# A two-layer adapter and feed-forward kernel: the second gate/up tile as seven block products instead of full ones

## The chip, the cores and the metric

The kernel runs on one core of one Trainium2 chip. The metric is the device time of one execution in microseconds (us), lower is better; a run's figure is the median of several executions. TensorE multiplies matrices into PSUM (eight banks of 128 x 512 float32), VectorE and ScalarE work elementwise on SBUF and PSUM, GpSimd works elementwise on SBUF and issues the gathers, and SyncE issues most of the other DMAs. Each engine takes its own list of instructions strictly in order and waits on semaphores for the others.

## What is computed

Two layers act on x, 8 x 128 tokens of width 512, in float32:

```python
def reference(x, itok_B_0_7, itok_B_3_7, ...):
    x = x + _L0_ffn_ref(_L0_cond_ref(x, itok_B_0_7, ...), ...)   # part touched here: _L0_ffn_ref
    x = x + _L1_ffn_ref(_L1_cond_ref(x, L1_cond_weight, itok_B_3_7), ...)
    return x
...
def _L0_ffn_ref(x, qweight_gu, qzeros_gu, scales_gu, g_idx_gu, ...):
    w_gu = _dequant(qweight_gu, qzeros_gu, scales_gu, g_idx_gu)   # sc[g] * (wq - (zq[g] + 1)), 4 bits
    inter = jnp.einsum('bsh,hf->bsf', x, w_gu)
    gate, up = (inter[..., :INTER], inter[..., INTER:])           # INTER = 1376
    h = jax.nn.silu(gate) * up
    w_d = _dequant(qweight_down, qzeros_down, scales_down, g_idx_down)
    return jnp.einsum('bsf,fh->bsh', h, w_d)
```

`_L0_cond_ref` is a linear layer with two gated low-rank experts for each token; its result is called y below. Layer 1 has the same shape with unquantized weights.

## The kernel before

**Three matmuls for one.** Every float32 operand is kept as a rounded high part (suffix `_hi`, made by a ScalarE copy) and the rest (`_lo`, made by a VectorE subtraction from it). A product of a 128 x 128 weight tile with 512 tokens is three matmuls of 512 columns: hi x hi, hi x lo, lo x hi.

**Gate/up of layer 0.** The 1376 hidden features make 11 tiles of 128 (`FT0 = 11`), numbered 0 to 10. A tile's weights are 128 gate and 128 up columns against 512 inputs. Tiles in `PLAIN` (0 and 1) are full products: `gate(i)` and `up(i)`, 4 input blocks x 2 token halves x 3 matmuls = 24 each. Tiles in `BLOCK_TILES` (2 to 10) treat weights and y as 2 x 2 blocks and take seven block products (a Winograd scheme) where eight are needed: `y_p_1` to `y_p_7`, each 2 x 3 = 6 matmuls, 42 a tile. Their right operands are blocks of y or of four sums of y's blocks (`yt_hi`, `yt_lo`, numbered 1 to 4), their left ones blocks of the weights or of four sums, which GpSimd makes for each tile (`sums_gu(i)`, four additions of 128 x 256).

**What a block tile costs the other engines.** VectorE dequantizes the raw weights (`dequant_gu(i)`, line 1252), GpSimd makes the sums, ScalarE rounds them (`w_hi(i)`, two copies, 768 and 1024 columns), VectorE makes the low part (`w_lo(i)`, lines 1241 and 1121). While TensorE runs the products, ScalarE takes three snapshots of banks (`y_snap_1`, `_5`, `_2`), VectorE adds other banks to them (`y_c_11`, `y_c_12`, `y_c_22`, lines 1291, 1296, 1301), ScalarE applies silu, and VectorE multiplies the two token halves (`y_mul_1` line 1311, `y_mul_0` line 1306). `h_split(i)` makes the high (ScalarE) and low (VectorE) part of the hidden tile. A plain tile needs one silu and one `gate_times_up` (line 1281) for these. Banks alternate between 0 to 3 and 4 to 7. TensorE's order in a tile i is p1(i), p4(i-1), p5, p2, p6, p3, p7; p4(i-1) waits for `y_c_22(i-1)`, which stands behind p7(i-1), and p1(i) for `w_lo(i)`.

**Order by hand.** Each engine's list is written out in its own function: nothing reorders it. The four differences of y (lines 1342 to 1348) are made on VectorE from `y_raw`, ScalarE's copies of the banks in which y's four quarters were summed (`y_copy`), and split by `y_sum_hi` and `y_sum_lo`. Zero points arrive by gather (`zg`) and are added to the 4-bit values for groups of tiles (`add_zeros`, line 1225; `ZERO_PARTS`). Scales arrive by four gathers for each pair of tiles (`scales_gu(j)` for tiles 2j and 2j+1). GpSimd's list is gathers and additions in one order; a gather for a reused buffer waits for the dequantization that read it.

## Time and profile before

| | |
|---|---|
| median of 3 runs | 441.03 us (440.88 to 444.47) |
| the profiled execution's own time | 440.44 us |
| its span, first to last instruction | 438.6 us |
| busy: TensorE matmul / VectorE / ScalarE / GpSimd | 99% / 76% / 51% / 48% of the span |
| granted TensorE clock, mean | 1.000 |
| instructions | 5493, of them 1938 matmuls |

The profile is one execution. A row of its timeline gives an instruction's start and duration and, in brackets, how long its engine had sat idle and what ended that. Matmuls are pipelined: the ends are modelled (390 ns for one of 512 columns), and the distance from start to start is what one costs. On VectorE and ScalarE too the next instruction starts some 0.08 us before the end of the one ahead. GpSimd's spans are rough.

### The profile page before, as it was taken

The numbers are of one execution on the slowest core, as the hardware profiler recorded it, in microseconds if no ns is written. First come the engines' busy times: TensorE is split into PE (matmuls) and PEld (weight loads), VectorE is DVE, ScalarE is ACT, GpSimd is POOL, SyncE is SP. The second block draws the span as 40 slices with busy tenths as digits, with TensorE's granted clock in tenths as the row PEclk, the third lists the DMA queues.
The fourth block names the chain that finished last, engine by engine and source line by source line (L and its number), as shares of the span: only waits on it lengthen the run. The fifth ranks groups of instructions, "written<-read, shape, count | busy, mean of one in ns | idle before, by whom it ended". The sixth has DMA issues, their size and how long they took to land.

```text
span 438.6 us, 5493 instructions
## 1 busy us (share of the span) xinstructions
PE 434.4 (99%) x1938; PEld 354.9 (81%) x1938; DVE 334.1 (76%) x413; ACT 223.8 (51%) x301; POOL 209.8 (48%) x182
## 2 busy tenths in 40 slices
PE   8999999999999999999999999999999999999997
PEld 4788888887888888888888888888888888888886
DVE  4869998999888854646778568778687678999922
ACT  5407646655555443255667756466465654473200
POOL 0477978868888304300024787986987300000000
PEclk9999999999999999999999999999999999999999
DMA  8974044101226475675289427838469136986623
GB/s 287 242 240 132 1 131 150 50 1 19 25 24 156 108 250 230 251 277 191 97 284 374 158 95 231 295 134 277 166 220 306 54 114 263 369 278 189 224 94 143
DMA packets 29401, 78.20 MB, mean 178 GB/s; under 512 B 2432, under 2 KB 15888, under 8 KB 27712
## 3 DMA queue, kind: packets, MB, share of 16 engines
q1 hardware_dynamic: 25312, 66.07, 43.3%
q0 software_dynamic: 3488, 11.10, 9.4%
q10 hardware_dynamic: 576, 0.72, 0.5%
q8 instruction: 13, 0.21, 0.2%
q14 instruction: 12, 0.10, 0.1%
HBM read 57.15 MB, written 20.73 MB: 178 GB/s over the span
## 4 chain that ended last, share of the span: by engine, by line
PE 96%; DVE 2%; DMA 1%; issue 0%; ACT 0%; ACTq 0%; DVEq 0%
PE ps L1937 10%; PE ps L1939 10%; PE ps L1938 10%; PE ps L1682 8%; PE ps L1686 8%; PE ps L1683 8%; PE ps L1805 6%; PE ps L1807 6%; PE ps L1806 6%; PE ps L2052 5%; PE ps L2050 5%; PE ps L2051 5%; PE ps L1920 2%; PE ps L1918 2%; PE ps L1919 2%; DMA res<-in_xT 1%
## 5 line engine op out<-in xcount | busy, mean ns | idle before, releaser
L1937 PE MATMUL ps<-zt_hi,ring_hi 128*128 128x512 f32 x140 | 54.6, 390 | 0.0
L1939 PE MATMUL ps<-zt_hi,ring_lo 128*128 128x512 f32 x140 | 54.5, 389 | 0.0
L1938 PE MATMUL ps<-zt_lo,ring_hi 128*128 128x512 f32 x140 | 54.5, 389 | 0.0
L760 ACT ACTIVATE ring_hi<-raw 128x1792 fp32r<-128x1792 f32 (+2 forms) x32 | 38.7, 1237 | 19.4 <-PE ps L1939 10.2
L1121 DVE TENSOR_TENSOR ring_lo<-raw,ring_hi 128x1024 fp32r<-128x1024 f32 (+3 forms) x24 | 42.4, 1771 | 6.9 <-ACT ring_hi L760 6.9
L1682 PE MATMUL ps<-h_hi,d_hi 128*128 128x512 f32 x88 | 34.2, 389 | 0.0
L1683 PE MATMUL ps<-h_lo,d_hi 128*128 128x512 f32 x88 | 34.2, 389 | 0.0
L670 POOL TENSOR_TENSOR raw<-raw 128x256 f32<-128x256 f32 x21 | 23.9, 1139 | 17.8 <-DMA raw<-in_gu 10.6
L1937 PEld LDWEIGHTS ps<-zt_hi,ring_hi 128*128 128x128 f32 x140 | 26.3, 188 | 6.0 <-issue 0.4
L1939 PEld LDWEIGHTS ps<-zt_hi,ring_lo 128*128 128x128 f32 x140 | 26.3, 188 | 5.5
L1938 PEld LDWEIGHTS ps<-zt_lo,ring_hi 128*128 128x128 f32 x140 | 26.3, 188 | 5.4
L673 POOL TENSOR_TENSOR raw<-raw 128x256 f32<-128x256 f32 x21 | 30.3, 1442 | 0.0
L633 POOL DMA_INDIRECT scale<-in_sc_gu,idx_gu x20 | 26.4, 1322 | 7.2 <-issue 5.3
L1805 PE MATMUL ps<-yt_hi,ring_hi 128*128 128x512 f32 x72 | 28.1, 390 | 0.2 <-DVE snap L1301 0.2
L1686 PE MATMUL ps<-h_hi,w_dn_lo 128*128 128x512 f32 x88 | 28.1, 389 | 0.0
L1807 PE MATMUL ps<-yt_hi,ring_lo 128*128 128x512 f32 x72 | 28.0, 389 | 0.0
L1806 PE MATMUL ps<-yt_lo,ring_hi 128*128 128x512 f32 x72 | 28.0, 389 | 0.0
L2052 PE MATMUL ps<-slot,wd 128*128 128x512 f32 (+1 forms) x73 | 27.8, 380 | 0.0
L2050 PE MATMUL ps<-slot,wd 128*128 128x512 f32 (+1 forms) x73 | 27.8, 380 | 0.0
L676 POOL TENSOR_TENSOR raw<-raw 128x256 f32<-128x256 f32 x21 | 26.1, 1245 | 3.0
L727 POOL TENSOR_TENSOR ad_lo<-ad_raw,ad_hi 128x1024 fp32r<-128x1024 f32 x1 | 2.4, 2405 | 48.6 <-ACT ad_hi L760 48.6
L1530 DVE TENSOR_TENSOR res<-ps,res 128x512 f32<-128x512 f32 (+1 forms) x18 | 10.8, 641 | 15.4 <-PE ps L2052 15.4
(254 smaller groups left out, 1199.8 us busy)
## 6 DMA issues: line engine op xcount, KB each, us to landing
ad_raw<-in_w1T SPq DMA_DIRECT2D x8, 1024.0 KB, 4.7
wd<-down_weights SPq DMA_DIRECT2D x7, 1024.0 KB, 5.5
down_weights<-dhi SPq DMA_DIRECT2D x7, 896.0 KB, 4.6
down_weights<-dlo SPq DMA_DIRECT2D x7, 896.0 KB, 4.1
raw<-in_gu SPq DMA_DIRECT2D x12, 512.0 KB, 3.6
wd<-down_weights SPq DMA_DIRECT2D x7, 768.0 KB, 5.5
draw<-in_d SPq DMA_DIRECT2D x7, 512.0 KB, 4.5
res<-in_xT SPq DMA_DIRECT2D x1, 2048.0 KB, 7.7
```

What stands on the lines that cost most here:

```text
L1121: dve.tensor_tensor(dst, src, hi_part.bitcast(F32), ALU.subtract).then_inc(done_sem, 1)
L1682: pe.matmul(ps[:, bank + hf, :], w_hi, v_hi[:, t], start=first, stop=False)
L1683: pe.matmul(ps[:, bank + hf, :], w_hi, v_lo[:, t], start=False, stop=False)
L1686: ins = pe.matmul(ps[:, bank + hf, :], w_lo, v_hi[:, t], start=False, stop=last)
L1805: pe.matmul(ps[:, bank, :], w_hi, v_hi, start=first_in_bank and k == 0, stop=False, skip_group_check=True)
L1806: pe.matmul(ps[:, bank, :], w_hi, v_lo, start=False, stop=False, skip_group_check=True)
L1807: ins = pe.matmul(ps[:, bank, :], w_lo, v_hi, start=False, stop=k == 1, skip_group_check=True)
L1937: pe.matmul(ps[:, bank, :], ring1_hi[s][:, w], z_hi[:, t], start=first and k == 0, stop=False, skip_group_check=True)
L1938: pe.matmul(ps[:, bank, :], ring1_hi[s][:, w], z_lo[:, t], start=False, stop=False, skip_group_check=True)
L1939: ins = pe.matmul(ps[:, bank, :], ring1_lo[s][:, w], z_hi[:, t], start=False, stop=k == 1, skip_group_check=True)
L2050: pe.matmul(ps[:, bank, c], w_hi, v_hi[:, c], start=k == LAST_K if bank != own else k == 0 and i in (1, 2, 3, 5), stop=False, skip_group_c ...
L2052: return pe.matmul(ps[:, bank, c], w_lo, v_hi[:, c], start=False, stop=k == DH - 1 or (n == 6 and m == 1 and k == LAST_K - 1), skip_group_ ...
```

## The change

Tile 1 moves from `PLAIN` to `BLOCK_TILES`. TensorE runs p1, p2, p5, p6, p3, p7 of tile 1 where `gate(1)` and `up(1)` stood, and its p4 behind p1(2). The weights of tile 1 need sums, so GpSimd gets `sums_gu(1)`; the differences of y, their parts, the combination of tile 1's banks and its multiplications are put in front of tile 2. Around that:

- `add_zeros` for tiles 5 to 10 was one instruction ahead of y's differences; it is now two (tiles 5, 6 and tiles 7 to 10), in the loop of tiles 2 and 3.
- The low part of hidden tile 0 moves into tile 2's loop on VectorE.
- The first adapter low part (`hg_lo`) is made ahead of the first `add_zeros`, and the last two gathers of `scale0` are issued behind the four of `zg`.
- ScalarE splits tile 1's weights behind the last split of y instead of behind the first; VectorE's `w_lo(1)`, `dequant_gu(3)` and the parts of y's sums are in another order. The two added waits on `s_yt` guard a snapshot buffer that shares memory with `y_raw`.
- On GpSimd `scales_gu(4)` waits for four zero parts and stands behind `sums_gu(5)`.

```diff
-BLOCK_TILES = tuple(range(2, FT0))
+BLOCK_TILES = tuple(range(1, FT0))
 NS = len(BLOCK_TILES)
...
 S_COL = {B_S1: 8 * P, B_S2: 10 * P, B_S3: 12 * P}
-PLAIN = (0, 1)
+PLAIN = (0,)
 NPAIRS = FT0 // 2
...
         nib = region(116, "nib", [P, FT0 * 2 * P], F32)
-        sil = {i: region(kb, f"sil{i}", [P, T], F32) for i, kb in zip(PLAIN, (100, 104))}
+        sil = {i: region(kb, f"sil{i}", [P, T], F32) for i, kb in zip(PLAIN, (100,))}
         y_raw = region(184, "y_raw", [P, KD, T], F32)
...
-        ZERO_PARTS = ((0, 2), (2, 5), (5, FT0))
+        ZERO_PARTS = ((0, 2), (2, 5), (5, 7), (7, FT0))
         m16 = nib.bitcast(U16).rearrange("p (i g w) -> p i g w", i=FT0, g=2 * KD)
...
             sp.wait_ge(s_zk, 32)
-            sp.wait_ge(s_ring, len(PLAIN))
+            sp.wait_ge(s_ring, 2)
             sp.dma_start(nib_dn[:, :], a["qw_dn"]).then_inc(s_qd, 16)
...
             pool.wait_ge(s_idx, 2)
-            scale_part(0, 0)
-            for k in range(1, KD):
+            for k in range(2):
                 scale_part(0, k)
...
                 gather(zg[:, 4 * ZW * k:4 * ZW * (k + 1)], kept_z, idx_gu[:, 0, k:k + 1], s_zg)
+            for k in range(2, KD):
+                scale_part(0, k)
...
             scales_gu(1)
+            sums_gu(1)
             scales_gu(2)
...
             sums_gu(4)
+            sums_gu(5)
             pool.wait_ge(s_n, len(ZERO_PARTS))
             scales_gu(4)
-            sums_gu(5)
+            sums_gu(6)
             scales_gu(5)
-            sums_gu(6)
             sums_gu(7)
...
                 act.wait_ge(s_p[1], frame(i) + 1)
+                if i == BLOCK_TILES[0]:
+                    act.wait_ge(s_yt, 3)
                 need(act, s_hm0, frame(i) - 1)
...
                 act.wait_ge(s_p[5], frame(i) + 1)
+                if i == BLOCK_TILES[0]:
+                    act.wait_ge(s_yt, 4)
                 need(act, s_hm1, frame(i) - 1)
...
             y_split(0, 0)
-            w_hi(1)
             y_split(1, 4)
...
             y_split(3, 2)
+            w_hi(1)
             y_copy(3, 2, KD)
...
             y_sum_hi(2)
+            y_sum_hi(3)
             w_hi(2)
-            y_sum_hi(3)
-            y_sum_hi(4)
-            h_split(0)
-            silu(1)
             for i in BLOCK_TILES:
                 y_snap_1(i)
-                if i + 1 < FT0:
+                if i == BLOCK_TILES[0]:
+                    y_sum_hi(4)
+                elif i + 1 < FT0:
                     w_hi(i + 1)
...
                 y_snap_5(i)
-                h_split(i - 1)
+                if i > BLOCK_TILES[0]:
+                    h_split(i - 1)
                 y_snap_2(i)
+                if i == BLOCK_TILES[0]:
+                    h_split(0)
                 y_silu_0(i)
...
                 i0, i1 = ZERO_PARTS[part]
-                dve.wait_ge(s_nib, 2 if i1 == FT0 else 1)
+                dve.wait_ge(s_nib, 2 if i1 > 5 else 1)
                 dve.tensor_tensor(m16[:, i0:i1], m16[:, i0:i1], zg16[:, i0:i1], ALU.add).then_inc(s_n, 1)
...
+            dve.wait_ge(s_hghi, 1)
+            lo(hg_lo, hg_full, hg_hi, s_hglo)
             dve.wait_ge(s_zg, 16 * KD)
             add_zeros(0)
-            dve.wait_ge(s_hghi, 1)
-            lo(hg_lo, hg_full, hg_hi, s_hglo)
             dequant_gu(0)
...
             y_split(0, 0)
-            w_lo(1)
             y_split(1, 4)
...
             dequant_gu(2)
-            y_split(2, 6)
-            y_split(3, 2)
-            dequant_gu(3)
-            add_zeros(2)
             b11, b12 = y_raw[:, 0:2, first], y_raw[:, 0:2, second]
...
             dve.tensor_tensor(y_low(yt_raw, 1), b12, b11, ALU.subtract).then_inc(s_yt, 1)
+            y_split(2, 6)
+            y_split(3, 2)
+            w_lo(1)
             dve.wait_ge(s_yr, KD)
...
             dve.tensor_tensor(y_low(yt_raw, 3), b22, b12, ALU.subtract).then_inc(s_yt, 1)
+            y_sum_lo(1)
             dve.wait_ge(s_yt, 2)
             dve.tensor_tensor(y_low(yt_raw, 4), b21, y_low(yt_raw, 2), ALU.subtract).then_inc(s_yt, 1)
-            y_sum_lo(1)
+            dve.wait_ge(s_yt, 4)
             y_sum_lo(2)
+            dequant_gu(3)
+            y_sum_lo(3)
             gate_times_up(0)
             w_lo(2)
-            y_sum_lo(3)
+            y_c_11(1)
             y_sum_lo(4)
-            h_split(0)
-            for i in BLOCK_TILES:
+            y_c_12(1)
+            y_c_22(1)
+            y_mul_1(1)
+            for i in BLOCK_TILES[1:]:
                 if i + 2 < FT0:
                     dequant_gu(i + 2)
-                if i > 2:
-                    y_mul_0(i - 1)
-                else:
-                    gate_times_up(i - 1)
+                y_mul_0(i - 1)
                 if i + 1 < FT0:
...
                 y_c_11(i)
+                if i == 2:
+                    h_split(0)
+                if i == 3:
+                    add_zeros(3)
                 h_split(i - 1)
...
                 y_mul_1(i)
+                if i == 2:
+                    add_zeros(2)
                 if i == 9:
...
                 weights_ready(i)
-                if i < 4:
-                    pe.wait_ge(s_hm, i - 1)
+                if i == 2:
+                    pe.wait_ge(s_hm, 1)
                 need(pe, s_hm0, frame(i) - 1)
...
             up(0)
-            weights_ready(1)
             pe.wait_ge(s_yr, KD)
-            gate(1, range(KD))
-            up(1)
-            for i in BLOCK_TILES:
+            y_p_1(1)
+            y_p_2(1)
+            y_p_5(1)
+            y_p_6(1)
+            y_p_3(1)
+            y_p_7(1)
+            for i in BLOCK_TILES[1:]:
                 y_p_1(i)
-                if i > BLOCK_TILES[0]:
-                    y_p_4(i - 1)
+                y_p_4(i - 1)
                 y_p_5(i)
...
                 y_p_6(i)
```

**GpSimd, from the zero stores on.** `raw0_1` and `raw0_0` are the weights of odd and even tiles: the first block of additions is `sums_gu`. Before:

```order
L633 DMA scale0<-in_sc_gu,idx_gu 128x512 x4
L633 DMA zg<-zeros_gu,idx_gu 128x704 x4
L633 DMA scale1<-in_sc_gu,idx_gu 128x512 x4
L633 DMA scale2<-in_sc_gu,idx_gu 128x512 x4
L670 ISA
L670 TENSOR_TENSOR raw0_0<-raw0_0 128x256
L671 TENSOR_TENSOR raw0_0<-raw0_0 128x256
L673 TENSOR_TENSOR raw0_0<-raw0_0 128x256
L676 TENSOR_TENSOR raw0_0<-raw0_0 128x2x128
```

After:

```order
L633 DMA scale0<-in_sc_gu,idx_gu 128x512 x2
L633 DMA zg<-zeros_gu,idx_gu 128x704 x4
L633 DMA scale0<-in_sc_gu,idx_gu 128x512 x2
L633 DMA scale1<-in_sc_gu,idx_gu 128x512 x4
L671 ISA
L671 TENSOR_TENSOR raw0_1<-raw0_1 128x256
L672 TENSOR_TENSOR raw0_1<-raw0_1 128x256
L674 TENSOR_TENSOR raw0_1<-raw0_1 128x256
L677 TENSOR_TENSOR raw0_1<-raw0_1 128x2x128
L633 DMA scale2<-in_sc_gu,idx_gu 128x512 x4
L671 TENSOR_TENSOR raw0_0<-raw0_0 128x256
```

The four additions of tile 1 now stand between the gathers of `scale1` and `scale2`, and tile 2's come behind both.

**VectorE, from y's differences to the first multiplication of a block tile.** `yt_raw` are the differences, `sil0` is `gate_times_up(0)`, `ring0_lo0` is the low part of tile 2's weights. Before:

```order
L1252 SCALAR_TENSOR_TENSOR raw0_1<-nib,scale1 128x1024
L1225 TENSOR_TENSOR nib<-nib,zg 128x3072
L1342 TENSOR_TENSOR yt_raw<-y_raw 128x1024
L1345 TENSOR_TENSOR yt_raw<-y_raw,yt_raw 128x1024
L1346 TENSOR_TENSOR yt_raw<-y_raw 128x1024
L1348 TENSOR_TENSOR yt_raw<-y_raw,yt_raw 128x1024
L1121 TENSOR_TENSOR yt_lo<-yt_raw,yt_hi 128x1024 x2
L1281 TENSOR_TENSOR sil0<-sil0,ps 128x1024
L1241 TENSOR_TENSOR ring0_lo0<-raw0_0,ring0_hi0 128x768
L1121 TENSOR_TENSOR ring0_lo0<-raw0_0,ring0_hi0 128x1024
L1121 TENSOR_TENSOR yt_lo<-yt_raw,yt_hi 128x1024 x2
```

After, from the first part of a difference to tile 1's `y_c_22` (`snap0_1` is tile 1's snapshots; differences 2 and 3 stand just ahead):

```order
L1129 TENSOR_TENSOR yt_lo<-yt_raw,yt_hi 128x1024
L1355 TENSOR_TENSOR yt_raw<-y_raw,yt_raw 128x1024
L1129 TENSOR_TENSOR yt_lo<-yt_raw,yt_hi 128x1024
L1260 SCALAR_TENSOR_TENSOR raw0_1<-nib,scale1 128x1024
L1129 TENSOR_TENSOR yt_lo<-yt_raw,yt_hi 128x1024
L1289 TENSOR_TENSOR sil0<-sil0,ps 128x1024
L1249 TENSOR_TENSOR ring0_lo0<-raw0_0,ring0_hi0 128x768
L1129 TENSOR_TENSOR ring0_lo0<-raw0_0,ring0_hi0 128x1024
L1299 TENSOR_TENSOR snap0_1<-ps,snap0_1 128x512
L1129 TENSOR_TENSOR yt_lo<-yt_raw,yt_hi 128x1024
L1304 TENSOR_TENSOR snap0_1<-ps,snap0_1 128x512
L1309 TENSOR_TENSOR snap0_1<-ps,snap0_1 128x512
```

`dequant_gu(3)` (`raw0_1<-nib,scale1`) has moved in between the parts, and the combinations of tile 1 (`snap0_1<-ps`) behind the low part of tile 2.

**VectorE in tile 2.** `ring0_lo1` is the low part of tile 3. Before:

```order
L1281 TENSOR_TENSOR sil1<-sil1,ps 128x1024
L1241 TENSOR_TENSOR ring0_lo1<-raw0_1,ring0_hi1 128x768
L1121 TENSOR_TENSOR ring0_lo1<-raw0_1,ring0_hi1 128x1024
L1291 TENSOR_TENSOR snap0_0<-ps,snap0_0 128x512
L1121 TENSOR_TENSOR h_lo<-sil1,h_hi 128x1024
L1296 TENSOR_TENSOR snap0_0<-ps,snap0_0 128x512
L1301 TENSOR_TENSOR snap0_0<-ps,snap0_0 128x512
```

After:

```order
L1314 TENSOR_TENSOR h_raw<-snap0_1,ps 128x512
L1249 TENSOR_TENSOR ring0_lo1<-raw0_1,ring0_hi1 128x768
L1129 TENSOR_TENSOR ring0_lo1<-raw0_1,ring0_hi1 128x1024
L1299 TENSOR_TENSOR snap0_0<-ps,snap0_0 128x512
L1129 TENSOR_TENSOR h_lo<-sil0,h_hi 128x1024
L1129 TENSOR_TENSOR h_lo<-h_raw,h_hi 128x1024
L1304 TENSOR_TENSOR snap0_0<-ps,snap0_0 128x512
L1309 TENSOR_TENSOR snap0_0<-ps,snap0_0 128x512
L1319 TENSOR_TENSOR h_raw<-snap0_0 128x512
L1233 TENSOR_TENSOR nib<-nib,zg 128x1024
```

The low part of hidden tile 0 (`h_lo<-sil0`) stands ahead of that of tile 1, and the zeros of tiles 5 and 6 at the end.

## Rows read from the trace of the kernel before

**Rows 1.** Page: busy time by engine; chain that ended last by engine

```profile
PE 434.4 (99%) x1938; PEld 354.9 (81%) x1938; DVE 334.1 (76%) x413; ACT 223.8 (51%) x301; POOL 209.8 (48%) x182
...
PE 96%; DVE 2%; DMA 1%; issue 0%; ACT 0%; ACTq 0%; DVEq 0%
```

**Rows 2.** Waits of TensorE: operation, releaser, us, times, longest

```profile
PE ps L1693 <- DVE zeros L1123: 1.2, 1, 1.2
PE ps L1805 <- DVE snap L1301: 0.2, 1, 0.2
```

**Rows 3.** Timeline, TensorE: start, duration, engine, line, operation, out<-in, count

```profile
42.11 0.39 PE L1682 MATMUL ps<-h_hi,ring_hi 128*128 128x512 f32 x1
...
52.99 0.39 PE L1682 MATMUL ps<-h_hi,ring_hi 128*128 128x512 f32 x1
...
63.87 0.39 PE L1805 MATMUL ps<-h_hi,ring_hi 128*128 128x512 f32 x1
...
65.23 0.39 PE L1805 MATMUL ps<-yt_hi,ring_hi 128*128 128x512 f32 x1
```

**Rows 4.** Timeline, all engines, at TensorE's one wait in the gate/up loop

```profile
101.51 0.67 DVE L1301 TENSOR_TENSOR snap<-ps,snap 128x512 f32<-128x512 f32 x1
...
101.72 0.39 PE L1807 MATMUL ps<-h_hi,ring_lo 128*128 128x512 f32 x1
...
102.33 0.47 PE L1805 MATMUL ps<-yt_hi,ring_hi 128*128 128x512 f32 x1 [0.21 <-DVE snap L1301]
```

**Rows 5.** Timeline, VectorE, no GpSimd addition beside it

```profile
31.17 0.69 DVE L1225 TENSOR_TENSOR nib<-nib,zg 128x1024 uint16<-128x1024 uint16 x1 [1.02 <-DMA zg<-zeros_gu,idx_gu]
...
39.98 0.95 DVE L1225 TENSOR_TENSOR nib<-nib,zg 128x1536 uint16<-128x1536 uint16 x1
...
57.98 0.94 DVE L1241 TENSOR_TENSOR ring_lo<-raw,ring_hi 128x768 fp32r<-128x768 f32 x1
58.85 1.21 DVE L1121 TENSOR_TENSOR ring_lo<-raw,ring_hi 128x1024 fp32r<-128x1024 f32 x1
59.99 2.34 DVE L1121 TENSOR_TENSOR yt_lo<-yt_raw,yt_hi 128x1024 fp32r<-128x1024 f32 x2
...
69.36 0.68 DVE L1291 TENSOR_TENSOR snap<-ps,snap 128x512 f32<-128x512 f32 x1
69.96 1.21 DVE L1121 TENSOR_TENSOR h_lo<-sil,h_hi 128x1024 fp32r<-128x1024 f32 x1
...
81.75 0.69 DVE L1301 TENSOR_TENSOR snap<-ps,snap 128x512 f32<-128x512 f32 x1 [0.55 <-PE ps L1807]
```

**Rows 6.** Timeline, VectorE, with GpSimd additions beside it

```profile
51.23 1.75 DVE L1346 TENSOR_TENSOR yt_raw<-y_raw 128x1024 f32<-128x1024 f32 x1
52.90 1.76 DVE L1348 TENSOR_TENSOR yt_raw<-y_raw,yt_raw 128x1024 f32<-128x1024 f32 x1
54.58 2.35 DVE L1121 TENSOR_TENSOR yt_lo<-yt_raw,yt_hi 128x1024 fp32r<-128x1024 f32 x2
```

**Rows 7.** Timeline, GpSimd, gathers and additions

```profile
27.10 0.95 POOL L633 DMA_INDIRECT zg<-zeros_gu,idx_gu  x1 [0.30 <-issue]
...
35.54 1.77 POOL L633 DMA_INDIRECT scale<-in_sc_gu,idx_gu  x1 [1.73 <-DVE raw L1252]
...
40.11 1.64 POOL L633 DMA_INDIRECT scale<-in_sc_gu,idx_gu  x1 [0.30 <-issue]
42.27 0.74 POOL L670 TENSOR_TENSOR raw<-raw 128x256 f32<-128x256 f32 x1 [0.53 <-DVE raw L1252]
...
50.18 1.72 POOL L673 TENSOR_TENSOR raw<-raw 128x256 f32<-128x256 f32 x1
```

**Rows 8.** Timeline, ScalarE, copies of y and high parts

```profile
42.31 1.03 ACT L760 ACTIVATE h_hi<-ps 128x1024 fp32r<-128x1024 f32 x1 [0.27 <-PE ps L1686]
44.63 1.94 ACT L799 ACTIVATE y_raw<-ps 128x1024 f32<-128x1024 f32 x2 [1.29 <-DVE h_lo L1121]
...
65.92 1.78 ACT L760 ACTIVATE ring_hi<-raw 128x768 fp32r<-128x768 f32 x2
```

## Prediction

> **What bounds the kernel now.** I read the page first, then TensorE's waits, then the timelines of the four engines around the change. On the page the reader is to see that TensorE's matmuls cover 99% of the span and 96% of the chain that ended last [rows 1]. Its waits come to one at the start and one of 0.2 us in the loop over the gate/up tiles [rows 2]. In its timeline the two plain tiles start at 42.11 and 52.99, the first block tile at 63.87, and its second product at 65.23 [rows 3]: 96 matmuls in 21.76 us are 0.227 us each, a product of six is 1.36 us, seven products are 9.52 us. So a matmul taken out is worth 0.227 us if TensorE is then never kept waiting, and a wait that is put in costs its full length, since nothing behind it is slack. The question is whether VectorE can serve tile 1 in time.
>
> Three durations of VectorE, start to next start: 1.14 us for 1024 columns, 0.87 for 768, 0.60 for 512 [rows 5]. When GpSimd adds at the same time, the 1024-column subtraction of two SBUF tensors takes 1.67 to 1.68 instead of 1.14 [rows 6], and an addition that takes 0.74 alone takes 1.72 [rows 7]: each addition that meets such an instruction puts 0.54 us on VectorE's list. I call that a hit. VectorE is not idle much: in a block tile it waits some 0.55 us for the last product [rows 5] and a few tenths elsewhere.
>
> **Part 1: what TensorE saves.** 48 matmuls become 42: 6 x 0.227 = **-1.36 us**. Nothing else leaves TensorE's list.
>
> **Part 2: when TensorE needs what.** `up(0)` is over at 52.99. Then p1(1) 52.99, p2 54.35, p5 55.71, p6 57.07, p3 58.43, p7 59.79, p1(2) 61.15, p4(1) 62.51. p4(1) waits for `y_c_22(1)`, p1(2) for `w_lo(2)`.
>
> **Part 3: VectorE up to p4(1).** The start is fixed by ScalarE: the last split of y runs at 42.31 as before, behind TensorE [rows 8]. Behind it now stand `w_hi(1)`, 1.78 us as tile 3's takes [rows 8], and the two copies of y, 1.94 us, which in before ran from 44.63: 43.3 + 1.7 + 1.9 = 46.9. So difference 2 starts at 47.0. From there the list has seven instructions of 1.14 (differences 2, 3 and 4, parts 1 and 2, `dequant_gu(3)`, part 3), 0.14 for one that waits for its own engine, `gate_times_up(0)` 1.13, `w_lo(2)` 0.87 + 1.14, `y_c_11` 0.60, part 4 1.14, `y_c_12` 0.60: 47.0 + 13.6 = 60.6. `y_c_22(1)` cannot start before p7(1) is complete, at 61.3, and with its 0.69 ends at 62.0. TensorE answers 0.15 us behind its end (102.18 to 102.33, [rows 4]): 62.2 against 62.51. Without hits tile 1 is just in time; VectorE can take up to 1.0 us more, two hits.
>
> How many there are: in before, tile 2's additions ran at 42.27 right behind `dequant_gu(2)` [rows 7]. Now `sums_gu(1)` goes first, from 35.5 to about 39.3 (three at 0.7 and one that is met, 1.7), then four gathers, 6.2 us as from 35.54 to 41.75 in before [rows 7], perhaps 7.2: `sums_gu(2)` starts between 45.6 and 46.9, on top of differences 2, 3, part 1 and difference 4, and takes 1.7 us for each. That is 3 to 4 hits. `sums_gu(3)` starts when `dequant_gu(3)` ends, 56.2, one addition beside `gate_times_up`, which reads PSUM and isn't met, the rest across `w_lo(2)`: 1 to 1.5 hits. With 5.3 hits, 2.9 us, `y_c_22(1)` starts at 63.5 and ends at 64.1; p4(1) starts at 64.3 and not 62.51: **+1.8 us** (0.2 of it ahead of p1(2), whose weights end at 61.2 against 61.15). Bounds: none (two hits), +3.2 (eight).
>
> Here a page bears on the size of a hit. The Trainium skill, SBUF — State Buffer, on how its two sides work, says that VectorE with two SBUF inputs and GpSimd share a port pair by an exclusive lock, the winner keeping it "for the whole instruction". By that each addition would block VectorE for its full 0.74 us, an estimate of 0.2 us more for each of the eleven hits of parts 3 and 4, and my sum would end at up to +4.5 us. The rows say 0.54 us, and I go by them.
>
> **Part 4: tiles 2 and 3.** In tile 2's loop VectorE has, from one `y_c_22` to the next: `y_mul_1` 0.61, `dequant_gu(4)` 1.14, `y_mul_0` 0.61, `w_lo(3)` 2.01, `y_c_11` 0.60, low part of hidden tile 0 1.14 (new here), of tile 1 1.14, `y_c_12` 0.60, `y_c_22` 0.69, and 0.36 of short waits: 8.9 us against TensorE's 9.52. `sums_gu(4)`, behind four gathers and starting near 67.8, meets three and a half of them: 10.85, **+1.3 us**. In tile 3's loop the zeros come on top: tiles 5 and 6, 1024 columns, 0.61; tiles 7 to 10, 2048 columns, 1.12 by the step from 0.69 to 0.95 us for 512 more [rows 5]; no second hidden part. 8.9 - 1.14 + 0.61 + 1.12, less 0.2 of a wait that they cover, is 9.3 us, and with 2.4 hits 10.56: **+1.0 us**. Bounds: 0 (no more than one hit in each) and +1.5, +1.9 (four in each). In before those zeros were one instruction ahead of the differences of y, where TensorE was busy with full tiles. From tile 4 on a loop has 7.8 us of work and its hits again, and the lag of VectorE is gone. With it goes the wait of before in tile 5 [rows 4]: 0.61 us between two matmuls for 0.227, and 0.07 behind it, **-0.45**.
>
> **Part 5: the rest at nothing.** `hg_lo` ahead of the first zeros: the zeros land at 31.17 in before [rows 5], now two gathers earlier, but the input of `hg_lo` is ready at 31.3; the first dequantization moves by 0.1 to 0.2 us, hidden because TensorE reads tile 0 from 42.11. The last gather of `scale0` takes the place of the last of `zg`, issued at 27.10 and landed at 31.17 [rows 5, 7], 4.1 us: it lands near 31.2 and is needed at 33.1. Without that cover of 1.9 us each us costs one. The snapshots' waits for the differences: the last ends at 53.8, the third snapshot waits for p5, 57.2. SyncE's list is the same. `scales_gu(4)` is needed in tile 6 and issued in tile 3.
>
> **Sum.** -1.36 + 1.8 + 1.3 + 1.0 - 0.45 = +2.3 us on the profiled execution's 440.44, 442.7. That execution is 0.6 below the median of the timed runs; on the median, 441.03, it is **443.3 us**.
>
> **The rivals.**
> - **Full gain.** GpSimd's additions slip so that at most two meet VectorE before p4(1), and at most one in each of the next two tiles. It speaks for it that without hits every deadline is met; against it that in before four in a row met y's differences, and that `sums_gu(2)` now lies wholly behind `scales_gu(2)`. Decides: `y_c_22(1)` ending by 62.4. Time: -1.36 - 0.45, 439.2 us. Chance 0.12.
> - **The change does nothing that can be seen.** Tile 1 is late as worked out, tiles 2 and 3 catch up because the additions fall beside reads of PSUM: -1.36 + 1.8 - 0.45 = 0, 441.0 us (with one of the two late, up to 442). Chance 0.2.
> - **The gathers are late.** The last of `scale0` lands behind 33.1 because the DMA queue is busier there or `zg` waits for its table's store, and VectorE's whole list moves, with 1:1 effect on p1(2) and p4(1). For it: four steps of four gathers are now tighter packed; against it: 1.9 us of slack. Or hits cost the page's full length, or all twelve additions hit (+3.2 + 1.5 + 1.9 - 1.8 = +4.8). Time 444.8 to 447, say 445.8. Chance 0.13.
>
> **How the numbers follow.** My forecast, 442 to 444.7 around 443.3, has 0.55. The range leaves out part of the full gain and the far end of the late gathers: 439.8 to 446. About 1% is what a measurement of this kernel can tell from no change, 4.4 us: slower than 445.4 needs most of the third rival, 0.09; faster than 436.6 is beyond what the six matmuls hold, 0.01; within it 0.9.
>
> **What would show it.** In TensorE's waits of the profile after: entries for the products behind VectorE's `y_c_22` in tiles 1, 2 and 3, some 1.6, 1.3 and 1.0 us, and a small one for `w_lo(2)`. In VectorE's timeline: differences 2 to 4 and part 1 at 1.7 us each and starting near 47.0; GpSimd's second block of additions from about 46 to 52.6. In tile 5: no wait. It is wrong if p4(1) starts by 62.7, if the second block of additions ends before 47, or if TensorE waits in front of `gate(0)` or `up(0)`.

## The result, and the profile after

The changed kernel takes 446.62 us (median of 6 runs, 444.73 to 447.16), the kernel before beside it 441.12: the ratio is 1.0106, 95% interval 1.0083 to 1.0128. The profiled execution took 446.57 us with a span of 444.8, against 440.44 and 438.6: 6.1 us more where 2.3 were forecast, and outside the range. The direction was right, the six matmuls are gone, and most of what was not foreseen happened before tile 1 and in tile 5. The ratios in this document leave out two executions that were far slower than all others, one of 627.62 us and one of 1137.07 us.

The page after: busy time by engine (us, share of the span, instructions), the granted clock, and the chain that ended last. Against [rows 1] TensorE has six matmuls fewer and nearly the same busy time, and VectorE's share of the chain went from 2% to 9%.

```profile
PE 434.3 (98%) x1932; PEld 353.4 (79%) x1932; DVE 338.9 (76%) x419; ACT 226.1 (51%) x306; POOL 210.6 (47%) x186
...
PEclk9999999999999999999999999999999999999999
...
PE 80%; DVE 9%; DMA 4%; issue 4%; POOL 2%; ACT 1%; SPq 0%; DVEq 0%; ACTq 0%
```

TensorE's waits (releaser, us in total, times, longest), which answer to [rows 2]: one wait of 0.2 us on `y_c_22`'s line has become four of 4.3 us in all, and two new ones stand beside them.

```profile
PE ps L1819 <- DVE snap L1309: 4.3, 4, 1.5
PE ps L1696 <- DVE h_lo L1129: 1.5, 1, 1.5
...
PE ps L1819 <- issue: 0.6, 1, 0.6
```

TensorE's timeline at the places where it waited, two rows for each (columns as in [rows 3]); the last is tile 5, [rows 4] before. For the second wait no releaser is named; `w_lo(2)`, which p1(2) needs, ends at 63.60, 0.1 before it.

```profile
44.33 0.61 PE L1700 MATMUL ps<-h_hi,ring_lo 128*128 128x512 f32 x2
46.46 0.50 PE L1696 MATMUL ps<-h_hi,ring_hi 128*128 128x512 f32 x1 [1.52 <-DVE h_lo L1129]
...
62.70 0.39 PE L1821 MATMUL ps<-yt_hi,ring_lo 128*128 128x512 f32 x1
63.70 0.47 PE L1819 MATMUL ps<-h_hi,ring_hi 128*128 128x512 f32 x1 [0.61 <-issue]
...
64.93 0.40 PE L1821 MATMUL ps<-h_hi,ring_lo 128*128 128x512 f32 x1
66.68 0.47 PE L1819 MATMUL ps<-yt_hi,ring_hi 128*128 128x512 f32 x1 [1.35 <-DVE snap L1309]
...
107.49 0.39 PE L1821 MATMUL ps<-h_hi,ring_lo 128*128 128x512 f32 x1
108.45 0.47 PE L1819 MATMUL ps<-yt_hi,ring_hi 128*128 128x512 f32 x1 [0.57 <-DVE snap L1309]
```

From here on the *loss* of a wait is the distance between the starts of two matmuls less the 0.227 us that a matmul takes anyway. The trace after has 1.68 in `gate(0)` (44.55, the second matmul of the first row, to 46.46), 0.77 before p1(2), 1.52 before p4(1), 1.67 in tile 2 (76.07 to 77.97), 0.98 in tile 3 (87.35 to 88.56) and 0.73 in tile 5: 7.35 us. The trace before has one, 0.38 in tile 5. Six times the matmul behind a wait runs slower too (66.68 to 66.98, 0.30 for 0.227): 0.4 to 0.5 us more. 7.35 - 0.38 - 1.36 + 0.4 = 6.0 us, which is the difference of the spans, 6.2, but for 0.2.

GpSimd's timeline shows where the first of these losses comes from. The stores of the two zero tables are issued, two gathers of `scale0` follow, and then the queue stands until the second store has landed; only behind the four gathers of `zg` come the last two of `scale0`.

```profile
16.35 0.72 POOL L647 DMA_DIRECT2D zeros_gu<-zu  x1 [15.89 <-DVE zu L1169]
17.06 0.56 POOL L648 DMA_DIRECT2D zeros_dn<-zu  x1
...
19.45 0.99 POOL L633 DMA_INDIRECT scale<-in_sc_gu,idx_gu  x1 [0.30 <-issue]
24.26 1.77 POOL L633 DMA_INDIRECT zg<-zeros_gu,idx_gu  x1 [3.82 <-DMA zeros_dn<-zu]
...
28.84 0.94 POOL L633 DMA_INDIRECT zg<-zeros_gu,idx_gu  x1 [0.30 <-issue]
...
31.98 0.95 POOL L633 DMA_INDIRECT scale<-in_sc_gu,idx_gu  x1 [0.30 <-issue]
```

VectorE's timeline: the zeros start at 33.18 and not at 31.17 as in [rows 5], the dequantization at 35.57 behind another wait for a gather, y's third and fourth low part at 45.18, the second difference at 50.03 and not near 47.

```profile
33.18 0.69 DVE L1233 TENSOR_TENSOR nib<-nib,zg 128x1024 uint16<-128x1024 uint16 x1 [2.32 <-DMA zg<-zeros_gu,idx_gu]
35.57 2.36 DVE L1260 SCALAR_TENSOR_TENSOR raw<-nib,scale 128x1024 f32<-128x1024 uint8 x2 [1.70 <-DMA scale<-in_sc_gu,idx_gu]
...
45.18 2.35 DVE L1129 TENSOR_TENSOR h_lo<-ps,h_hi 128x1024 fp32r<-128x1024 f32 x2
...
50.03 1.76 DVE L1351 TENSOR_TENSOR yt_raw<-y_raw,yt_raw 128x1024 f32<-128x1024 f32 x1
51.71 1.76 DVE L1352 TENSOR_TENSOR yt_raw<-y_raw 128x1024 f32<-128x1024 f32 x1
53.38 1.76 DVE L1129 TENSOR_TENSOR yt_lo<-yt_raw,yt_hi 128x1024 fp32r<-128x1024 f32 x1
55.07 1.21 DVE L1355 TENSOR_TENSOR yt_raw<-y_raw,yt_raw 128x1024 f32<-128x1024 f32 x1
```

### The profile page after: what moved, and what is told of

Read it like the earlier page. It is cut to its first block, busy times and chain, and to the rows that moved or that the text cites. A ratio compares the mean times of both kernels' runs of the same rounds, so it can differ in the third digit from the quotient of the medians.

```text
span 444.8 us, 5513 instructions
## 1 busy us (share of the span) xinstructions
PE 434.3 (98%) x1932; PEld 353.4 (79%) x1932; DVE 338.9 (76%) x419; ACT 226.1 (51%) x306; POOL 210.6 (47%) x186
## 4 chain that ended last, share of the span: by engine, by line
PE 80%; DVE 9%; DMA 4%; issue 4%; POOL 2%; ACT 1%; SPq 0%; DVEq 0%; ACTq 0%
PE ps L1953 10%; PE ps L1955 10%; PE ps L1954 10%; PE ps L1696 5%; PE ps L1700 5%; PE ps L1697 5%; PE ps L2068 5%; PE ps L2067 5%; PE ps L2066 5%; PE ps L1819 5%; PE ps L1821 5%; PE ps L1820 4%; DMA res<-in_xT 2%; DVE h_lo L1129 2%; PE ps L1936 2%
## 5 line engine op out<-in xcount | busy, mean ns | idle before, releaser
L671 POOL TENSOR_TENSOR raw<-raw 128x256 f32<-128x256 f32 x22 | 26.8, 1219 | 20.4 <-DMA raw<-in_gu 10.4
L1819 PE MATMUL ps<-yt_hi,ring_hi 128*128 128x512 f32 x80 | 31.5, 393 | 4.3 <-DVE snap L1309 4.3
L1820 PE MATMUL ps<-yt_lo,ring_hi 128*128 128x512 f32 x80 | 31.2, 390 | 0.0
L1821 PE MATMUL ps<-yt_hi,ring_lo 128*128 128x512 f32 x80 | 31.2, 390 | 0.0
L633 POOL DMA_INDIRECT scale<-in_sc_gu,idx_gu x20 | 25.4, 1269 | 5.6 <-issue 5.3
L674 POOL TENSOR_TENSOR raw<-raw 128x256 f32<-128x256 f32 x22 | 27.9, 1266 | 0.0
L677 POOL TENSOR_TENSOR raw<-raw 128x256 f32<-128x256 f32 x22 | 25.2, 1144 | 3.2
L672 POOL TENSOR_TENSOR raw<-raw 128x256 f32<-128x256 f32 x22 | 24.5, 1114 | 0.0
```

The lines of the kernel that those rows point to most:

```text
L1819: pe.matmul(ps[:, bank, :], w_hi, v_hi, start=first_in_bank and k == 0, stop=False, skip_group_check=True)
L1820: pe.matmul(ps[:, bank, :], w_hi, v_lo, start=False, stop=False, skip_group_check=True)
L1821: ins = pe.matmul(ps[:, bank, :], w_lo, v_hi, start=False, stop=k == 1, skip_group_check=True)
```

## The experiments

Theory A: the time is the sum of the forecast's terms (VectorE's list with its hits in tiles 1, 2 and 3) and of one that was put at nothing, the gathers, which now wait for a store. Theory B: hits or the length of the list do it all, and the early wait only takes time that would be lost in tile 1 anyway. Ratios are to the kernel before, run on the same chip.

### Order of the gathers undone (e1_order, e5_own_wait, e2_before_order)

```
-            for k in range(2):
+            for k in range(KD):
                 scale_part(0, k)
             pool.wait_ge(s_zk, 32)
...
-            for k in range(2, KD):
-                scale_part(0, k)
```

> The changed kernel with one edit undone: the four gathers of scale0 stand again ahead of the wait for the stores of the zero tables, the four of zg behind it. Theory A (the gathers were late because zg waits for its table's store, and scale0 parts 2 and 3 now stand behind that wait): the first dequantization starts at 32.9 and not 35.57, the wait of 1.7 us inside gate(0) is gone, the second difference of y starts near 47 and not at 50.03; then what was predicted for tiles 1 to 3 is left, 2.5 to 3.5 us over the kernel before, 2 to 3 us below the changed one. Theory B (the GpSimd additions alone make VectorE late, the early wait only takes time that TensorE would lose in tile 1 anyway): the wait in gate(0) goes, the one for the product behind y_c_22 in tile 1 grows by as much, and the time is within 0.5 us of the changed kernel, 5 to 6 us over the kernel before.

Measured: 444.40 us, ratio 1.0060 (1.0020 to 1.0099); span 442.6. `gate(0)` has no wait, the dequantization starts at 33.45, and the losses are 0.30 and 1.52 in tile 1, 1.65, 0.95 and 0.73 in tiles 2, 3 and 5. VectorE's first dequantization, then its list from the second difference on, and one of GpSimd's additions of tile 2 beside it:

```profile
33.45 2.36 DVE L1258 SCALAR_TENSOR_TENSOR raw<-nib,scale 128x1024 f32<-128x1024 uint8 x2
...
47.87 1.76 DVE L1349 TENSOR_TENSOR yt_raw<-y_raw,yt_raw 128x1024 f32<-128x1024 f32 x1
48.51 1.71 POOL L672 TENSOR_TENSOR raw<-raw 128x256 f32<-128x256 f32 x1
49.56 1.76 DVE L1350 TENSOR_TENSOR yt_raw<-y_raw 128x1024 f32<-128x1024 f32 x1
51.23 1.76 DVE L1127 TENSOR_TENSOR yt_lo<-yt_raw,yt_hi 128x1024 fp32r<-128x1024 f32 x1
52.92 1.21 DVE L1353 TENSOR_TENSOR yt_raw<-y_raw,yt_raw 128x1024 f32<-128x1024 f32 x1
...
63.72 0.67 DVE L1307 TENSOR_TENSOR snap<-ps,snap 128x512 f32<-128x512 f32 x1
```

This is the list of Part 3: a start at 47.87 (47.0 forecast), three full hits on the differences and part 1, `y_c_22(1)` at 63.72 (63.5 forecast), and a loss of 1.82 in tile 1 where 1.8 was forecast. The sum agrees better than its parts. From 47.87 to 63.72 are 15.85 us, the bare 13.6 and 2.25 of hits, where 2.9 were forecast; and the list starts 0.9 late. ScalarE's copies of y end at 47.35, but VectorE comes to the difference only behind `w_lo(1)` at 47.87, with a hit on it (1.76 for 1.21) that the prediction did not count.

The second kernel keeps the changed order and gives the first store, that of zg's table, a semaphore of its own, so that zg waits for that store alone.

```
-            pool.wait_ge(s_zk, 32)
+            pool.wait_ge(s_zk1, 16)
```

> The changed kernel, order of gathers as changed, but zg waits only for the store of its own table, the first of the two stores, which lands 4.9 us behind its issue, where the second lands 6.9 us behind its own; the second is waited for ahead of the first gather that reads it. Theory A: zg starts near 21.3 and not 24.26, scale0's last gather is issued near 29.2, the first dequantization starts near 33, and the time is that of the kernel with the old order within 0.5 us, 2 to 3 us below the changed kernel. A rival (the queue is simply busier there, the landing of a gather and not the wait decides): the dequantization starts after 34.5 and the time falls by less than 1 us.

Measured: zg starts at 22.65, the dequantization at 32.97, `gate(0)` has no wait, and the profiled execution takes 444.28 us, that of e1_order 444.40; so in these traces the wait for the store made the dequantization late, not a busier queue. But the median is 445.58, ratio 1.0082 (1.0044 to 1.0121), 1.2 us above e1_order's: the time within 0.5 us of it was missed. The traced execution was the fastest of the five, and the first store does not always land so early (last section).

This trace shows one thing more. The additions of tile 2 started earlier, at 44.88, and fell on `w_lo(1)` and not on the differences, which take 1.21 us each. `w_lo(1)` took the hits instead (the row is its first part, 0.94 without them), the second difference started only at 49.44, though ScalarE's copies of y ended at 46.9, and tile 1 loses 0.30 and 1.51 us, as in e1_order (0.30 and 1.52). So it is VectorE's own list ahead of the second difference, hits included, and not ScalarE that fixes its start.

```profile
44.85 2.98 DVE L1252 TENSOR_TENSOR ring_lo<-raw,ring_hi 128x768 fp32r<-128x768 f32 x1
```

The third is the kernel before with only this part of the change.

> The kernel before with only the first part of the change: scale0 parts 2 and 3 gathered behind zg, and the low part of hg ahead of the first zeros. Theory A: zg then waits for the stores until about 24, VectorE dequantizes at 35.5 and not 32.9, y's third low part starts near 44 and not 42.1, and TensorE waits 0.8 us inside gate(0); nothing more, since tile 1 is plain and y's differences have time: 0.5 to 1.2 us over the kernel before. Theory B (the gathers' order costs nothing by itself): within 0.3 us of the kernel before.

Measured: 440.63 us, ratio 0.9976 (0.9940 to 1.0013). The dequantization starts at 34.26, 1.35 later than in the trace before and not 2.6, and TensorE waits nowhere in `gate(0)`. Both numbers of theory A were missed: 34.26 is still early enough for this kernel. Here y's third low part starts 9.05 us behind the dequantization, in the changed kernel 9.6 behind it, 0.55 more: there `sums_gu(1)` hits the zeros of tiles 2 to 4 (1.51 us for 0.95).

### The two orders on one chip (h1_after_again, i3_after, i4_order)

> The changed kernel itself once more, beside the others on one chip and with a second trace. If the late first dequantization is regular and not one execution's, gate(0) waits again: by 1 to 2.5 us, as much as the first dequantization starts behind about 33.9 (35.57 and 1.68 us in its first trace, 35.98 and 2.2 us in the run with the additions first, 33.45 and none with the old order). Time 4 to 6 us over the kernel before.

> The changed kernel a third time, to be set against the next one on the same chip. Its two traces so far differ in one wait: 1.68 us in gate(0) in the first, none in the second, where scale0 landed a microsecond earlier. Median 445 to 446.5 us.

> The changed kernel with the old order of gathers, a second time and beside the changed one. If the gathers' order is a term of its own in the time and not only in single traces, it is 0.8 to 2.2 us below the kernel of the run before this one; if it is under 0.4 us, the miss of the prediction lies with tiles 1 to 5 alone.

Measured: the changed kernel 445.46 (ratio 1.0098, 1.0062 to 1.0133) and 445.90 (1.0110, 1.0084 to 1.0136); the old order beside the latter 444.64 (1.0073, 1.0058 to 1.0088): 1.3 us less, the intervals touch. So theory A holds for the time too, with 1.3 us for the order of the gathers. The wait of 1 to 2.5 us in `gate(0)` that was expected of h1_after_again is not in its trace. What single traces show is set by when the stores land, which is not the same from one execution to the next:

| trace | first zg gather | first dequantization | loss in `gate(0)` |
|---|---|---|---|
| e1_order (old order) | 24.29 | 33.45 | 0 |
| h1_after_again (changed) | 24.01 | 34.52 | 0 |
| i3_after (changed) | 24.12 | 35.24 | 1.48 |
| changed, first trace | 24.26 | 35.57 | 1.68 |
| i4_order (old order) | 25.76 | 35.67 | 1.62 |
| e3_sums2_first (old order) | 26.28 | 35.98 | 1.98 |

In the kernels with the changed VectorE list each microsecond of the dequantization behind about 33.9 costs one in `gate(0)` (in h1_after_again TensorE itself was 0.6 us later, with the last matmul ahead of p1(2) at 61.64 and not at 61.03 as in e1_order, which is why 34.52 was in time). With one and the same landing the changed order is 1 to 2 us later; with a landing 1.5 to 2 us later the old order loses as much. GpSimd's first gather of zg and VectorE behind it, in i4_order:

```profile
25.76 1.34 POOL L633 DMA_INDIRECT zg<-zeros_gu,idx_gu  x1 [2.71 <-DMA zeros_dn<-zu]
...
34.94 0.69 DVE L1231 TENSOR_TENSOR nib<-nib,zg 128x1024 uint16<-128x1024 uint16 x1 [3.96 <-DMA zg<-zeros_gu,idx_gu]
35.67 2.36 DVE L1258 SCALAR_TENSOR_TENSOR raw<-nib,scale 128x1024 f32<-128x1024 uint8 x2
```

### Hits in tile 1 (e3_sums2_first, f1_wait_and_sums2)

Both kernels have the old order of gathers, f1_wait_and_sums2 also the wait for the first store alone. To these the additions of tile 2 are moved:

```
+            sums_gu(2)
             scales_gu(2)
-            sums_gu(2)
```

> The changed kernel with the old order of gathers, and with GpSimd's additions of tile 2 ahead of its four gathers of scale2 and not behind them. If the hits of these additions on y's differences are what makes tile 1 late (four of 0.54 us): the additions run from about 42.3 to 46, beside VectorE instructions that read PSUM, the second difference starts near 47 and takes 1.14 us, TensorE's wait for the product behind y_c_22 in tile 1 falls from some 1.6 us to under 0.3, and the time is 1.3 to 2 us below that of the kernel with the old order of gathers alone; the waits of tiles 2 and 3 stay near 1.3 and 1.0 us or grow by some tenths. If the length of VectorE's list and not the hits makes tile 1 late, the time moves by less than 0.5 us.

Measured: 442.84 us, ratio 1.0031 (0.9993 to 1.0070); the profiled execution was the one with the latest landing, 445.18 us, with 1.98 lost in `gate(0)`, but its differences take 1.21 each and tile 1 loses 0.72 although they start at 50.39. The median is 1.6 us below e1_order's, as expected.

> The changed kernel with the old order of gathers, zg waiting for its own table's store alone, and the additions of tile 2 ahead of the gathers of scale2. The run with these additions first lost 1.98 us in gate(0) again, because the two stores landed at 25.98 there and not at 23.99 as in the run with the old order alone. If that late landing was all that hid the gain of the fewer hits, gate(0) has no wait here, the second difference starts near 47.5 and takes 1.14, y_c_22(1) ends by 62.6, and tile 1 costs at most 0.3 us; tiles 2, 3 and 5 keep 1.65, 0.95 and 0.73 us: 1.4 to 1.9 us below the kernel with the old order alone, 2 to 2.6 over the kernel before. If tile 1's lateness is the length of the list, p4(1) waits a microsecond still and the gain is under 0.6 us.

Measured: 442.79 us, ratio 1.0037 (1.0013 to 1.0060). No wait in `gate(0)`, losses 0.47, 1.65, 0.95 and 0.73. Tile 1 falls from 1.82 to 0.47 (0.3 expected): its lateness was the hits. In the other traces with these additions moved it loses 0.31 to 0.77, so the move is worth 1.0 to 1.5 us; f3_small_adds and f4_nibbles_tile4, which lose nothing there, are not counted, since one has shortened additions and the other a TensorE 4 us late. Two of the four additions now run beside low parts that read PSUM, and neither engine's instruction is longer:

```profile
42.75 2.35 DVE L1130 TENSOR_TENSOR h_lo<-ps,h_hi 128x1024 fp32r<-128x1024 f32 x2
43.39 0.74 POOL L673 TENSOR_TENSOR raw<-raw 128x256 f32<-128x256 f32 x1
```

### What tiles 2 and 3 cost (f3_small_adds, f2_list_even)

In the changed kernel's trace three additions of tile 4 lie inside one low part of VectorE in tile 2, and the fourth meets the next:

```profile
71.68 0.79 POOL L671 TENSOR_TENSOR raw<-raw 128x256 f32<-128x256 f32 x1
71.99 2.96 DVE L1129 TENSOR_TENSOR h_lo<-sil,h_hi 128x1024 fp32r<-128x1024 f32 x1
...
73.08 0.78 POOL L674 TENSOR_TENSOR raw<-raw 128x256 f32<-128x256 f32 x1
74.87 1.75 DVE L1129 TENSOR_TENSOR h_lo<-h_raw,h_hi 128x1024 fp32r<-128x1024 f32 x1
```

Both experiments start from f1_wait_and_sums2. The first makes the additions of tiles 3, 4 and 5 short and leaves their sums unfinished, so it shows times only.

```
-                sums(sum_at("q", i), *blocks0(i % 2))
+                b = blocks0(i % 2)
+                sums(sum_at("q", i), *((t[:, :, 0:8] for t in b) if i in (3, 4, 5) else b))
```

> The first kernel of this call with GpSimd's additions of tiles 3, 4 and 5 done on 16 of 256 columns each (their block sums are left unfinished, so products of these tiles are not those of the reference). It shows tiles 1 to 3 without hits. If hits are half of the lateness of tiles 2 and 3 (3.5 and 2.4 of 0.54 us), the list alone, 8.9 and 9.3 us, fits into 9.52, and TensorE's waits in tiles 1 to 3 are gone (under 0.3 us in all); what is left is tile 5, 0.73 us: 439.5 to 440.3 us. If the list alone is too long, 0.8 us or more of waits are left in tiles 2 and 3.

Measured: 439.70 us, ratio 0.9962 (0.9939 to 0.9985), 3.1 us less than with the full additions. One wait is left in the loop, tile 5's 0.74. So without the hits of three tiles' additions nothing of the 3.07 us that f1_wait_and_sums2 lost in tiles 1 to 3 is left, and the change is worth 1.1 us on the medians; the bare lists of 8.9 and 9.3 us do fit into 9.52.

```
             w_lo(0)
+            for part in range(1, len(ZERO_PARTS)):
+                add_zeros(part)
...
-                if i == 2:
+                if i == 3:
                     h_split(0)
```

> The kernel of the run before this one, and VectorE's small work put elsewhere: all zeros are added right behind w_lo(0), where VectorE waited in the kernel before, and the low part of hidden tile 0 is moved from tile 2's loop to tile 3's (its region moved by 4 KB). If tiles 2 and 3 are late because of the length of VectorE's list in them (Part 4 of the prediction), tile 2 loses 1.14 of its 1.65 us and tile 3 gives 1.73 for 1.14: TensorE's waits fall to 0.3 to 0.8 and 0.2 to 0.6 us, 1.2 to 2 us below the run before, 0.3 to 1 us over the kernel before or equal to it; the zeros make y's splits at most 0.5 us late. If the hits alone decide there, whatever the list, the time moves by less than 0.5 us.

Measured: 442.82 us, ratio 1.0043 (1.0015 to 1.0070). Tile 2's loss went from 1.65 to 0 and tile 3's from 0.95 to 0.39, 2.2 us together. Tile 2's list is shorter by 1.14 us and meets one hit less (the low part that took 1.75 is gone from behind the long one); tile 3's is 0.6 shorter with nearly the same hits. So the length of the list counts as well as the hits: what a tile loses is both together beyond 9.52. But the zeros at w_lo(0) made `gate(0)` lose 1.30 and 0.52, not 0.5 in all, and tile 1 0.76: they were paid in another place. The gain expected did not come.

### Tile 5 (f4_nibbles_tile4, i2_before_nibbles4, g3_sums7_first)

f4_nibbles_tile4 starts from f2_list_even, i2_before_nibbles4 from the kernel before, g3_sums7_first from f1_wait_and_sums2. The *nibbles* are VectorE's splitting of the packed weights of the down product (`nibbles_dn`).

```
-                if i == 5:
+                if i == 4:
                     nibbles_dn()
```

> The second kernel of this call with the nibbles of the down weights split in tile 4's loop and not in tile 5's. Tile 4 has 1.25 us in which VectorE waits for TensorE, tile 5 has none and lost 0.73 us. If tile 5's wait is the sum of this 0.87 us and the additions that fall on its low parts, it is gone here and tile 4 has none: 0.6 to 0.8 us below the second kernel, at or just under the kernel before (0.99 to 1.001). If the additions alone make it (in the changed kernel they start behind the gathers of scale_last, on h_lo, which takes 2.84 us), 0.4 us or more of the wait stays.

Measured: tile 5's wait is gone and tile 4 has none, but the time is 443.08 us, ratio 1.0046 (1.0019 to 1.0072), no gain. The trace has 2.32 lost in `gate(0)`, and behind that wait TensorE's granted clock fell. The table of stretches (us and length, TensorE busy and matmuls, granted clock, DMA share, GB/s):

```profile
42.00:44.00 2.00, 0.10 (x1) 1.00 0.00 0
44.00:46.00 2.00, 1.75 (x6) 0.72 0.00 0
46.00:48.00 2.00, 2.00 (x6) 0.50 0.00 0
48.00:50.00 2.00, 2.00 (x9) 0.92 0.00 0
50.00:60.00 10.00, 10.00 (x45) 1.00 0.33 107
```

> The kernel before with one move: the nibbles of the down weights in tile 4's loop and not in tile 5's. If TensorE's wait in tile 5 (0.38 us beyond the matmul's own time) is the price of these nibbles on top of tile 5's hits, it is gone and no wait is put in its place in tile 4: 0.3 to 0.5 us below the kernel before. If it comes back in tile 4, no change.

Measured: 441.53 us, ratio 1.0016 (0.9994 to 1.0037). In the kernel before the same move takes tile 5's 0.38 away and puts 0.74 in tile 4. The wait came back in tile 4, where the additions hit as well, and there is no gain. How large the wait is depends on where the additions fall: in e2_before_order, whose kernel has tile 5 as the kernel before has it, they hit `w_lo` for 0.5 us and not 0.9, and tile 5 loses 0.06.

> The kernel with its own store's wait, old order of gathers and the additions of tile 2 first, and one thing more: GpSimd's additions of tile 7 stand ahead of the gathers of scale_last, not behind them. In the changed kernel they start at 103.9, behind those gathers, and three of them fall inside one low part of VectorE, which takes 2.84 us; in the kernel before they started at 93.97 as soon as their tile was dequantized, and TensorE waited 0.38 us in tile 5 and not 0.73. If that order is what made tile 5's wait grow, it is 0.4 us here or less and the time 0.3 to 0.7 us lower; if it is the nibbles of the down weights in that loop, it stays at 0.7.

Measured: tile 5 loses 0.37, as in the kernel before, so the growth to 0.73 was GpSimd's order: in the changed kernel the additions of tile 7 come behind the gathers of scale_last and fall on a low part of VectorE (first rows below, from the changed kernel's trace). But the time is 445.12 us, ratio 1.0087 (1.0056 to 1.0117): 1.49 and 1.21 are lost in tile 6. The gathers of scale_last stand behind these additions now, and VectorE waits 4.19 us for the last of them before it can dequantize tile 8 (last row, from g3_sums7_first); the additions of tile 8 start at 110.83 and not at 108.77 as in f1_wait_and_sums2.

```profile
102.82 1.06 POOL L633 DMA_INDIRECT scale_last<-in_sc_last,idx_gu  x1 [0.30 <-issue]
103.89 0.74 POOL L671 TENSOR_TENSOR raw<-raw 128x256 f32<-128x256 f32 x1
104.59 0.74 POOL L672 TENSOR_TENSOR raw<-raw 128x256 f32<-128x256 f32 x1
105.29 0.73 POOL L674 TENSOR_TENSOR raw<-raw 128x256 f32<-128x256 f32 x1
...
104.27 2.84 DVE L1129 TENSOR_TENSOR h_lo<-h_raw,h_hi 128x1024 fp32r<-128x1024 f32 x1
...
109.53 1.23 DVE L1261 SCALAR_TENSOR_TENSOR raw<-nib,scale 128x1024 f32<-128x1024 uint8 x1 [4.19 <-DMA scale_last<-in_sc_last,idx_gu]
```

### Versions meant to beat both (g4_even_sums7, g5_even_sums4, i1_sums4_zeros, j1_nibbles6)

> A version meant to beat both: that of the run before this one, with the low part of hidden tile 0 in tile 3's loop, the zeros of tiles 5 and 6 added together with those of tiles 2 to 4 ahead of y's differences, the last zeros (tiles 7 to 10) in tile 4's loop, where VectorE waited 1.25 us, and the nibbles of the down weights in tile 6's; scale4 is gathered behind the additions of tile 6. By the sums of VectorE's lists TensorE waits 0.5 us in tile 1, 0.5 in tile 2, 0.3 in tile 3 and none in gate(0), tiles 4 and 5: 440.2 to 441 us, ratio to the kernel before 0.997 to 1.001. If the early zeros make y's splits late (they cost 1.8 us in gate(0) when all of them stood there), 1 us more.

> The kernel before this one, and GpSimd's additions of tile 4 ahead of the gathers of scale3 and not behind them. Behind them three additions fell inside one low part of a hidden tile (2.96 us and not 1.22). Ahead of them they start as dequant_gu(4) ends and lie beside y_mul_0 and y_c_11, which read PSUM, and w_lo(3). If hits count by what VectorE instruction they meet, tile 2 has one or two fewer of them, its wait is gone and tile 3's is under 0.3 us: 0.4 to 1 us below the kernel before this one, ratio 0.995 to 0.999. If each addition costs VectorE its 0.54 us wherever it falls, no change.

Measured: 446.61 us (1.0123, 1.0086 to 1.0161) and 447.50 us (1.0130, 1.0084 to 1.0176), slower than the changed kernel (445.46 on the same chip), where 440.2 to 441 us was expected of the first and less of the second. Tiles 2 and 3 lose no more than was worked out (0 and 0.40; 0 and 0), but `gate(0)` loses 0.84 and 0.62, tile 4, where the zeros now stand, 0.41 and 0.45, and GpSimd's list is full behind tile 4. With gathers moved behind additions VectorE waited 5.66 us for one (the row below, from the second version; the first has the same wait), and TensorE lost 2.72 and 1.12 us in the first version, 2.72 and 2.70 in the second. The clock fell again: in the first behind the wait of 2.57 us, in the second only behind its second one (mean 0.995 in both).

```profile
108.74 1.22 DVE L1261 SCALAR_TENSOR_TENSOR raw<-nib,scale 128x1024 f32<-128x1024 uint8 x1 [5.66 <-DMA scale_last<-in_sc_last,idx_gu]
```

The third version keeps the additions of tile 4 first and leaves GpSimd's order behind tile 5 alone; the nibbles stand in tile 4's loop.

```
-            scales_gu(3)
             pool.dma_start(lnb[:, :], a["lnw"].partition_broadcast(P)).then_inc(s_ln, 16)
             sums_gu(4)
+            scales_gu(3)
...
-        ZERO_PARTS = ((0, 2), (2, 5), (5, 7), (7, FT0))
+        ZERO_PARTS = ((0, 2), (2, 7), (7, FT0))
```

> A second version meant to reach the kernel before: own store's wait, old order of gathers, additions of tile 2 ahead of the gathers of scale2 and those of tile 4 ahead of the gathers of scale3, zeros of tiles 5 and 6 with those of tiles 2 to 4, nibbles of the down weights in tile 4; the last zeros stay in tile 3, and GpSimd's order behind the additions of tile 5 is the changed kernel's. In the version before it the additions of tile 4, moved so, left VectorE idle in tile 2, and its loss of 2.7 us in each of tiles 6 and 7 came from GpSimd, whose gathers of scale_last landed only at 108.7. If that is so, there is no wait behind tile 4 here, and tiles 1, 2 and 3 wait 0.5, 0.6 and 0.2 us, gate(0) 0 to 0.8: 440.6 to 441.6 us, 0.999 to 1.002.

Measured: 441.34 us, ratio 1.0003 (0.9991 to 1.0015), losses 0.54, 0.37 and 0.37 in tiles 1 to 3, none behind tile 4 and none in `gate(0)`; but 0.72 in tile 4, with the nibbles. That is the time of i2_before_nibbles4 (441.53 beside it), which has its nibbles there too.

> The second version meant to reach the kernel before, with the nibbles of the down weights in tile 6's loop and not in tile 4's. In its trace VectorE waits for TensorE in tile 6 for 1.4 us in all (0.57, 0.67 and 0.17), in tile 4 not at all, and tile 4 lost 0.72 us. If these waits are room, the 0.87 us (1.4 with a hit) fit in, the wait is gone and the time is 0.5 to 0.8 us lower: 440.5 to 441, ratio to the kernel before 0.998 to 1.000. If each tile's room is eaten by hits as tile 4's was, 0.4 us or more comes back in tile 6.

Measured: 440.26 us (12 runs, 439.82 to 441.05), the kernel before beside it 440.88; ratio 0.9988, 0.9978 to 0.9999. Tiles 4, 5 and 6 have no wait, which was the expectation; 1.09 us is lost in all, in tiles 1, 2 and 3.

```profile
PE ps L1818 <- DVE snap L1310: 0.6, 3, 0.2
...
72.44 0.39 PE L1820 MATMUL ps<-h_hi,ring_lo 128*128 128x512 f32 x1
73.04 0.47 PE L1818 MATMUL ps<-yt_hi,ring_hi 128*128 128x512 f32 x1 [0.22 <-DVE snap L1310]
```

So with VectorE's and GpSimd's lists laid out anew the kernel is 0.6 us below the one before and some 5 us below the kernel as changed. That is a tenth of a per cent, and the interval just leaves out no change. It is not shown that the block products of tile 1 bring these 0.6 us. This version also moves the nibbles out of tile 5, where the kernel before loses 0.38 us and 0.07 behind it. In the sum of the traces the block products save 1.36 us and the waits left, with the slower matmuls behind them, cost 1.32, so nearly all of the gain is the wait of tile 5. A kernel before with its nibbles in tile 6 was not run.

## Why the prediction was wrong

The sum was +2.3 against +6.1 us. By its own steps:

- **Part 1, -1.36:** right. 1932 matmuls for 1938, and without hits (f3_small_adds) the kernel is 1.1 us faster than before on the medians.
- **Part 2, deadlines:** right; with no wait in `gate(0)` TensorE was ready for p4(1) at 63.0 in e1_order, which is 62.51, the 0.3 lost before p1(2) and 0.2 of small shifts.
- **Part 3, +1.8:** the cause was right, hits on VectorE's list; the size, 1.82 in e1_order, is partly luck. The list met 2.25 us of hits and not 2.9, and it began 0.9 late: "The start is fixed by ScalarE" was wrong, since VectorE's `w_lo(1)` stands ahead of it and took a hit that was not counted (in e5_own_wait tile 2's additions hit nothing but `w_lo(1)`, and tile 1 loses the same). In the changed kernel's trace it is 2.29, since the list came 3 us later than forecast and only part of that was lost in `gate(0)` already. f1_wait_and_sums2 took the hits away, and 1.35 of it went.
- **Part 4, tile 2 +1.3, tile 3 +1.0:** 1.67 and 0.98. Tile 3 was right; tile 2 was mis-sized by 0.4: three additions fell inside one low part, which took 2.96 for 1.21, and the next took 1.75, 2.3 us where 3.5 hits of 0.54 were counted as 1.9. The mechanism is shown by f3_small_adds (both terms gone) and f2_list_even.
- **Part 4, tile 5 -0.45:** wrong in sign, +0.35. The step that failed is "the lag of VectorE is gone. With it goes the wait of before". That wait is tile 5's own: nibbles and hits in one loop. A lag had nothing to do with it: in the trace before VectorE waits 0.29 us for TensorE ahead of `y_c_22(4)`, just before that loop. And GpSimd's new order put three additions on one low part there (g3_sums7_first gives the old 0.37 back; j1_nibbles6, with the nibbles elsewhere, takes it away).
- **Part 5, at nothing:** this is the step that failed most: "it lands near 31.2 and is needed at 33.1". It was found by putting each gather in the place of another, as if the queue never stood. In the kernel before, two more gathers of scale0 ran while the stores landed; without them GpSimd stands 3.82 us, and the last gather of scale0 is issued at 31.98 and not 27.10, so it could not land at 31.2. The need was near 33.9 rather than 33.1. It cost 1.68 us in `gate(0)` in the first trace and 0.5 more in tile 1; between the medians on one chip 1.3 us (i3_after against i4_order). The third rival names this wait ("`zg` waits for its table's store"), but the chance it got rested on a slack of 1.9 us that took no account of it; its 444.8 to 447 is where the time fell.
- **The sum** took 0.07 us for the slower matmul behind a wait once; six waits make 0.4 to 0.5.

Together: 1.7 + 0.5 (gathers), 0.8 (tile 5), 0.4 (tile 2), 0.4 (restarts) are 3.8 of the 3.8 us missed. Only the first trace is added up here; of the 2.2 us for the gathers the medians of two kernels show 1.3, and late landings cost the old order as much in single executions. Left open is why the second store lets zg go at 22.75 in one execution and at 26.28 in another; no run changed the traffic beside it.

The page's rule that was weighed: the Trainium skill, SBUF — State Buffer, on how its two sides work, has the winner of the port keep it "for the whole instruction", which would make a hit 0.74 us. In e1_order each full hit is 1.76 less 1.21, 0.55 us; in the changed kernel's trace three additions inside one low part are 2.96 less 1.21, 1.75 us, 0.58 each. The measured size decides; the up to +4.5 that the rule would give is nearer to the result, but by other terms.

## What to carry to other kernels

When gathers are reordered, look at what the queue waited for and did not have to: a wait that shows no idle time before may be covered by exactly the instructions that the change moves away, and its semaphore wait stands in the code even if no row of the trace shows it. When one engine's list serves another within a fixed time for each tile, write for every tile the list, the hits and the room; work moved out of one tile is paid in the next unless that one has room, and the trace shows the room as idle time with the served engine as its releaser. A second engine's instructions on the same memory cost by what they meet: moving four additions off instructions that read SBUF alone, in part onto some that read PSUM, was worth 1.0 to 1.5 us in tile 1. When a version with several edits comes out ahead, give the kernel before each edit that it can take as well, before the gain is put down to one of them.

## What the runs showed of the hardware

- Waits of TensorE of 1.82 us or less in the gate/up part left its granted clock at 1.0 in these traces. One of 2.15 us (f4_nibbles_tile4) was followed by matmuls 0.43 us apart, a granted clock of 0.50, the 1.2 GHz level, until 48.3, some 4 us after work resumed, and cost 1.7 us beyond the wait itself. A wait of 2.57 us lowered it in g4_even_sums7 (0.57 from 113 to 115), but one of the same length in g5_even_sums4 did not (1.00 from 113 to 115); there it fell behind the next wait, of 2.55 us, which began 3.0 us after work had resumed (0.50 from 119 to 121). So the length of one wait did not decide it.
- Three GpSimd additions in a row can run inside one VectorE subtraction of two SBUF tensors: they keep their 0.73 to 0.79 us each and the subtraction takes 2.84 to 2.96 for 1.21. When single additions meet such subtractions one after the other, both are longer (e1_order: 1.76 for 1.21 and 1.71 for 0.74). Beside VectorE instructions that read PSUM neither is slowed (f1_wait_and_sums2: 2.35 for two of 1024 columns, an addition of 0.74).
- The store of 11 KB to DRAM (`zeros_gu`) landed 3.8 us behind its issue in e3_sums2_first, 4.9 in the changed kernel's first trace, 5.5 in e5_own_wait and 8.4 in g4_even_sums7 (zg's start at 25.16 less 0.3, against 16.44). So a wait on such a store varied by 4.6 us between executions, and a kernel that only just covers it varies with it.
